# Eight block transfers replaced by two ScalarE copies in a gated delta rule kernel

## The reference

```
attn = -(einsum('bhcid,bhcjd->bhcij', k_beta, k) * decay_mask)   # 64x64 for each chunk and value head
attn = where(upper, 0, attn)                                     # strictly lower triangular
attn = scan(_correct_row, attn)                                  # rows 1..63: forward substitution
attn = attn + eye(64)                                            # = inverse of (1 - attn)
value_corrected = attn @ v_beta
for each chunk c:                                                # carries a 128x128 state
    v_prime = v_c - k_cumdecay_c @ state
    out_c   = (q_c @ state) * g_exp_c + intra_c @ v_prime
    state   = state * g_exp_last_c + (k_c * k_decay_c)^T @ v_prime
out = rmsnorm(out * silu(z)) @ W_out
```

## Time and profile before

| | |
|---|---|
| median of 3 runs | 4948.56 us (4940.16 to 4948.61) |
| the profiled execution | 4963.24 us |
| its span, from first to last instruction | 4961.4 us |
| TensorE matmuls | 4639.9 us busy, 94% |
| VectorE | 3576.3 us busy, 72% |
| ScalarE | 3063.8 us busy, 62% |
| GpSimd | 693.1 us busy, 14% |
| mean granted TensorE clock | 0.984 |

### The profile page before, as it was taken

The page is one execution under the profiler, slowest core; times in us unless marked ns, Lnnn a source line. Parts: engine busy times, 40 slices in busy tenths (PEclk is TensorE's granted clock), DMA queues, the critical chain, the costliest instruction groups (busy, mean ns, idle before and its releaser), DMA issues.

```text
span 4961.4 us, 144941 instructions
## 1 busy us (share of the span) xinstructions
PE 4639.9 (94%) x54288; PEld 3178.9 (64%) x54320; DVE 3576.3 (72%) x7576; ACT 3063.8 (62%) x7979; POOL 693.1 (14%) x680
## 2 busy tenths in 40 slices
PE   4898999999999899999999899999999999999998
PEld 2555666666666566666666666666666666666666
DVE  7554777777777677777777677777777777777776
ACT  2333666666666566666666566666666666666665
POOL 0000111111111111111111111111111111111111
PEclk8999999999999999999999999999999999999999
DMA  2111222222223222222223222222223232222221
GB/s 61 32 43 60 66 69 52 61 67 61 68 50 81 69 68 50 64 67 61 59 58 81 68 58 59 64 63 65 60 57 81 68 69 55 59 66 60 69 58 34
DMA packets 760100, 305.22 MB, mean 62 GB/s; under 512 B 672880, under 2 KB 716016, under 8 KB 749168
## 3 DMA queue, kind: packets, MB, share of 16 engines
q1 hardware_dynamic: 620144, 287.40, 23.6%
q10 hardware_dynamic: 139264, 8.42, 1.8%
HBM read 216.96 MB, written 66.07 MB: 57 GB/s over the span
## 4 chain that ended last, share of the span: by engine, by line
PE 71%; DVE 8%; ACT 6%; issue 6%; SPq 5%; DMA 4%; ACTq 0%; DVEq 0%; POOL 0%; POOLq 0%
PE pj L660 16%; PE dsb L819 8%; PE pj L655 7%; PE pod L803 4%; PE pot L777 4%; PE dsb L791 4%; PE ms L693 4%; PE pot L748 4%; PE pod L760 3%; PE pj L650 3%; ACT arena L983 2%; PE pot L605 2%; PE ms L673 2%; SPq L333 2%; PE ms L687 2%
## 5 line engine op out<-in xcount | busy, mean ns | idle before, releaser
L660 PE MATMUL pj<-xnT,wt 128*128 128x512 f32 x2048 | 1023.2, 623 | 29.3 <-DMA cw<-in_L_attn_conv_weight 15.7
L1292 DVE SCALAR_TENSOR_TENSOR cy<-xpad,cw,cy 128x1024 f32<-128x1024 f32 x768 | 981.3, 1278 | 10.4 <-ACT cy L1003 1.2
L1562 POOL TENSOR_TENSOR rout<-rin,expo 128x2 f32<-128x2 f32 x512 | 358.3, 700 | 3743.4 <-DVE rin L1443 3743.4
L819 PE MATMUL dsb<-wo,yT 128*128 128x256 f32 x2048 | 575.7, 404 | 17.9 <-issue 16.9
L660 PEld LDWEIGHTS pj<-xnT,wt 128*128 128x128 f32 x2048 | 352.2, 192 | 358.9 <-issue 343.9
L1429 DVE SCALAR_TENSOR_TENSOR st<-st,gel,dsb 128x128 f32<-128x128 f32 x1536 | 430.4, 343 | 207.7 <-PE dsb L791 202.8
L1002 ACT ACTIVATE xpad<-pj 128x512 f32<-128x512 f32 x512 | 304.9, 596 | 360.8 <-PE pj L660 360.8
L655 PE MATMUL pj<-wt,xnT 128*128 128x256 f32 x2048 | 510.0, 392 | 0.0
L1062 ACT ACTIVATE yT<-dsb 128x256 f32<-128x256 f32 x512 | 202.2, 395 | 491.2 <-PE dsb L810 489.5
L819 PEld LDWEIGHTS dsb<-wo,yT 128*128 128x128 f32 x2048 | 348.7, 190 | 123.2 <-issue 95.4
L655 PEld LDWEIGHTS pj<-wt,xnT 128*128 128x128 f32 x2048 | 368.9, 190 | 84.0 <-issue 44.3
(11 more groups left out here) (174 smaller groups left out, 8011.6 us busy)
## 6 DMA issues: line engine op xcount, KB each, us to landing
qge<-ge_rows SPq DMA_DIRECT2D x64, 1024.0 KB, 7.4
wt<-in_L_attn_W_qkvz SPq DMA_DIRECT2D x64, 768.0 KB
gb<-g_rows SPq DMA_DIRECT2D x128, 256.0 KB
a_d<-at SPq DMA_DIRECT2D x64, 512.0 KB, 2.6
wo<-in_L_attn_W_out SPq DMA_DIRECT2D x64, 256.0 KB, 2.7
x_d<-xpair SPq DMA_DIRECT2D x128, 128.0 KB, 1.8
ap_<-a_d SPq DMA_DIRECT2D x512, 16.0 KB, 1.8
dd<-x_d SPq DMA_DIRECT2D x512, 16.0 KB, 2.1
```

The lines of the kernel that those rows point to most:

```text
L660: last = mm(pj[n % 2][:, :], wt[:, k, col:col + DH], batch(xnT, k, i), start=(k == 0), stop=(k == KD - 1))
L819: last = mm(dsb[:, 0, GRP * DH:GRP * DH + D], yT[:, h, :], wo[:, p, h, :], start=(h == 0), stop=(h == GRP - 1))
L1292: stt(y, x[:, :, tap:tap + SEQ], cw[:, kind, tap:tap + 1], y, ALU.mult, ALU.add).then_inc(S["conv"], 1)
L1562: tt(rout[:, :], rin[:, :], expo[:, 0, 0:GRP], ALU.pow).then_inc(S["routs"], 1)
```

## The change

The eight transfers into `eturn` and their semaphore go. ScalarE fills `eturn` with two copies out of `ee` instead, each from one half of the partitions into the other, 8 units of 64. They stand at s = 19 between the second and the third negation, behind a wait for the transfers into `ee`, which ScalarE did not wait for until now. TensorE's round 0 waits for the copies in place of the transfers.

```diff
@@ relayout_back (SyncE)
                 blocks_back(sp, 0, dd, d_dd)
-                loaded(sp, d_x1, g, 1)
-                apart(sp)
-                for r in range(GRP * NBLK):
-                    turned = (r + NBLK) % (GRP * NBLK)
-                    sp.dma_start(eturn[turned * BLK:(turned + 1) * BLK, :, (r % NBLK) * BLK:(r % NBLK + 1) * BLK],
-                                 x_d[r * U + U // 2:(r + 1) * U, 1].rearrange("u j i -> j u i")).then_inc(d_et, 16)
@@ fixpoint (TensorE)
                     loaded(pe, d_ee, g, GRP * NBLK)
-                    loaded(pe, d_et, g, GRP * NBLK)
+                    after(pe, "turned", g, NB)
                     after(pe, "pneg", g, 2)
@@ ScalarE
+            def turned_blocks(g):
+                loaded(act, d_ee, g, GRP * NBLK)
+                for b in range(NB):
+                    fn(eturn[half(1 - b), :, :], ee[half(b), 8:16, :], ACT.Copy).then_inc(S["turned"], 1)
@@ front_piece (ScalarE)
-                for n in range(3):
-                    if s == 19:
-                        negated(g, n)
+                if s == 19:
+                    negated(g, 0)
+                    negated(g, 1)
+                    turned_blocks(g)
+                    negated(g, 2)
```

More of the change, by code:

```diff
@@ L205, in build @@
         d_w, d_g, d_ge, d_wo, d_q = sem("d_w"), sem("d_g"), sem("d_ge"), sem("d_wo"), sem("d_q")
-        d_a0, d_a, d_off, d_x0, d_x1, d_dd, d_ee, d_et = (sem(n) for n in ("d_a0", "d_a", "d_off", "d_x0", "d_x1", "d_dd", "d_ee", "d_et"))
+        d_a0, d_a, d_off, d_x0, d_x1, d_dd, d_ee = (sem(n) for n in ("d_a0", "d_a", "d_off", "d_x0", "d_x1", "d_dd", "d_ee"))
         phase = sem("phase")
@@ L231, in build @@
             counted(name, n)
-        for name, n in (("pcopy", RING), ("silu", 4), ("sqs", 2), ("dexp", 1), ("pneg", 3), ("wev", NC), ("wos", 1),
+        for name, n in (("pcopy", RING), ("silu", 4), ("sqs", 2), ("dexp", 1), ("pneg", 3), ("turned", NB), ("wev", NC), ("wos", 1),
                         ("sso", NC), ("yte", NC), ("ysc", NC)):
@@ L887, in _ @@
         def _(act):
-            starts(act, ("pcopy", "silu", "sqs", "dexp", "pneg", "wev", "wos", "sso", "yte", "ysc"))
+            starts(act, ("pcopy", "silu", "sqs", "dexp", "pneg", "turned", "wev", "wos", "sso", "yte", "ysc"))
             fn = nc.scalar.activation
```

## The result

| | before | after |
|---|---|---|
| median, measured in turn | 4944.36 us (6 runs, 4935.2 to 4953.43) | 4967.85 us (6 runs, 4951.0 to 4977.76) |
| ratio, 95% interval | | 1.0043 [1.0027, 1.0058] |
| span of the profiled execution | 4961.4 us | 4976.0 us |
| mean granted TensorE clock | 0.984 | 0.983 |

The change made the kernel 0.43% slower, by about 21 us, where 25 us less had been forecast. So the loss is small but stands.

A forecast was written before the change was run, and what follows sets the result against it. TensorE, busy 94% of the span, was taken as the bound, idling on eturn's transfers before the first round. Gains of 15.4 and 11.0 less 1.0 us gave 25, so 4924 us on the median; 8-in-10 range 4908 to 4952.

The forecast's parts named there:

- the moved wt load: SyncE's queue: next head's wt load issues 5 us earlier, beside the last ee blocks; no gain by itself.
- the sum: First-round starts over 64 heads: 15.4 + 11.0 - 1.0 + 0 = 25.4 us gained, taken as 25.
- rival 1: ee lands late behind wt, decisive beyond 2.3 us later; slower, 4958 to 4984 us; chance 0.10.
- ScalarE's wait for ee: New wait before the copies: least margin 1.6 us, median 2.3 over 64 heads, so no cost.
- The pair of copies: ScalarE, SBUF to SBUF: pair ends 1.05 us behind the second negation, bounds 0.96 and 1.26 us.
- The release: TensorE's way from released wait to the first round's first matmul: 0.34 us, 0.09 in the last 14 heads.
- rival 4: All idle time VectorE had before its residual goes: 33.7 us gained, 4915 us; chance 0.09.
- rival 3: Small gain: copies or release slower, or time waited out at TensorE's next stop; 4938 us up; 0.24 with rival 5.
- which wait stood in front of the first round: TensorE before the first round waits for eturn's transfers: 49.3 us idle in 40 waits.
- ScalarE's later work has cover: Work queued behind the copies comes 1.05 us later, covered by 3.29 us of ScalarE's idle time in head 7; no cost.
- rivals 2 and 5: 2: ScalarE becomes the bound, 67 us, 5016, chance 0.05; 5: transfers were hidden anyway, chance folded into rival 3.
- rival 5: The eturn transfers in front of the first round were hidden anyway; chance folded into rival 3, together 0.24.

The follow-up runs named there:

- e16: The changed kernel unaltered, run again on the chip of e17, against the kernel before: 4971.06 us, ratio 1.0041.
- e17: The changed kernel with wt issued at its old time, behind the second negation (e9 once more), against the kernel before: 4938.34 us, ratio 0.9982.
- e8: The changed kernel without ScalarE's copies and TensorE's wait for them, wt still early, part of the inverse left out, against the kernel before: 4951.82 us, 1.0019.
- e12: e9 without both copies and the wait for them, wt at its old time, against the kernel before: 4933.42 us, ratio 0.9967.
- e9: The changed kernel with wt held behind ScalarE's second negation, its old time, against the kernel before: 4929.6 us, ratio 0.9979.
- e2: The kernel before, eturn transfers kept, with wt issued between the dd blocks and eturn's, against the kernel before: 5064.42 us, ratio 1.0227.
- e1: The changed kernel with SyncE issuing wt only once the ee blocks have landed, against the kernel before: 4956.31 against 4950.22 us, ratio 1.002.
- e10: The kernel before with ScalarE's two copies added, into a tile nobody reads, eight transfers kept, against the kernel before: 4940.23 us, ratio 0.9993.

## Why the prediction was wrong

**The step that failed** is the moved wt load. The prediction says that "it moves forward by 5 us", that "the earlier load gains nothing by itself" and that this "is where this change could bite", and gives it no term in the sum. It has one: e16 against e17 prices it at +33 us, more than the whole forecast gain. It acts in two ways.

*The late ee blocks (rival 1).* The mechanism was named, with a chance of 0.10, and ScalarE's wait for ee was "costed at nothing". "wt lasts 3 us in all" was read as a reason against it; it is about the size of the delay. The last ee block of a head came 2.5 us later in the median, just past the rival's threshold of 2.3: 4.62 us with 768 KB beside it, 3.46 with 384, 2.0 with none. The Trainium skill, "DMA: Bandwidth & Descriptors", section "Queues, rings and completion order", has a DMA engine take turns between SP's and ACT's rings at packet borders only; the delays agree with blocks that stand behind wt's share. Their price is an estimate. By the idle time before the first round it is 11 us (e16 less e17). By the ratios it is 6 us (0.24% from e8 to the change, less 0.12% from e12 to e9), a difference that the intervals don't resolve.

*TensorE's pauses and its clock.* No rival spoke of them. Against e12, e8 has the same work and waits and only wt earlier: 1.0019 [1.0003, 1.0036] against 0.9967 [0.9953, 0.9982], 26 us, of which late ee blocks hold 1.2. TensorE stops at fixed places of the code: the pauses of over 1 us in pj<-dd,off stand in heads 3, 10, 11, 18, 19, 26, 27, 34, 35, 42 and 43, before and after the change alike, so at four heads of the loop's body of 16, pass after pass. They lasted 1.0 to 2.1 us before, 1.6 to 3.0 after, 1.0 to 1.8 in e9, 2.1 to 3.3 in e2. After the change, the granted clock went to 1.2 GHz behind 7 of the 9 that were over 2 us long; before, behind the 2 longest, of 2.09 us. The profile of before showed these waits, 18.1 us of them, and the prediction passed over them as they weren't eturn's.

*What TensorE waits for there* can be read from the DMA packets in the traces. The page of either kernel has a queue of instruction reads, 16 KB each:
```profile
q8 instruction: 455, 7.45, 0.6%
```
One such read comes for every 251 matmuls and weight loads of TensorE (median, before), and its pauses end with them. Over the 17 traces there are 328 pauses of TensorE of over 1 us, from 545 us on, without a releaser and in the middle of a batch or in pj<-dd,off. All 328 end 1.0 to 1.7 us behind the end of a read on this queue. By chance about one in ten would (an estimate: 436 reads in 4416 us). So, as far as the traces can tell, TensorE waits there for its own instructions. In pj<-dd,off the read starts 0.8 us ahead of the stop before (median), 0.8 to 1.0 in e1, e9, e12 and e17. It starts 0.0 us ahead of it after, 0.2 in e8 and e16, and 0.2 behind it in e2. In these four runs, with wt early, every one of the 42 reads starts between 0.7 us ahead of the end of wt's last packet and 0.2 us behind it, 3.7 to 4.4 us behind the issue of wt. In before and e17 all 21 start ahead of wt's issue, by 0.2 to 2.4 us. The early load thus holds up the read, TensorE stops for longer, and more often its clock falls.

**The pair of copies.** Forecast: ends 1.05 us behind the second negation, bounds 0.96 and 1.26. Measured: the pair takes 1.28 us and ends 1.30 us behind it where ee is there in time. In head 7 after:
```profile
1006.22 1.07 ACT L1032 ACTIVATE pbd<-ms 128x512 f32<-128x512 f32 x2
1007.32 1.28 ACT L1039 ACTIVATE eturn<-ee 64x512 f32<-64x512 f32 x2
...
1008.51 0.57 ACT L1032 ACTIVATE pback<-pj 128x512 f32<-128x512 f32 x1
```
From the negation's end at 1007.29 to 1008.60. The overlap of 0.1 us that two negations show does not come between the two copies, of 0.628 us each, nor between negation and copy, so the pair lies beyond my upper bound. It isn't the shape: the two activations of that shape in the earlier trace rows do overlap, in the kernel before.
```profile
161.63 0.63 ACT L926 ACTIVATE kq<-vT 64x512 f32<-64x512 f32 x1
162.16 0.61 ACT L927 ACTIVATE kq<-vT 64x512 f32<-64x512 f32 x1
```
Why the copies don't stays open. By the prediction's own method the longer pair alone takes 26.0 to 15.0 us; with ee 2.5 us later besides, 5.7 are left, still a gain. The release was right: the first matmul at 1008.95, 0.35 us later (0.34 forecast).

**What a microsecond at the first round is worth.** The sum took each as one microsecond of the kernel if VectorE could follow. e9 gave 0.2%, 10 us, of the 15; e12 gave 16 us for an idle time of 52, where rival 4, fed by what VectorE idled, had 33.7. The rest is idled again in rounds 1 and 2, as rival 3 said of "TensorE's next stop", but for the most part no other engine makes that stop: a TensorE that waits less comes sooner to the end of the instructions that it has. All pauses in the middle of a batch, over 0.2 us long, are 52.4 us in e12 and 20.7 in e9, and all 98 of them (72 and 26) end 1.0 to 1.75 us behind an instruction read. So even with wt in place the forecast of 25 would have been more than twice too high, and rival 3 would have come.

**Right:** which wait stood in front of the first round; that ScalarE's later work has cover (e10); that rivals 2 and 5 are out (rival 5 narrowly, as e9 gains 0.2%); the 128 activations, and wt issued 5 us earlier.

**The sum.** On the medians: -10 us for the freed wait (e9), +33 for the early load (e16 against e17), +23; measured +21 to +24. By the estimates above the 33 split into some 6 to 11 us for late ee blocks and 22 to 27 for the pauses and the clock.

**What stays open.** That TensorE's long pauses end behind instruction reads, and that the reads start only as wt's last packets end, is seen in every case of the traces. No run moved the code against the load or the reads to another time, so the order of cause rests on these times and on e16 against e17. Why the clock falls behind some pauses and not behind others of the same length isn't shown. Why halving wt at its old place gives 0.43% was not taken apart further; its profile has about 21 us less idle time from 545 us on, spread over many places.

## What to carry to other kernels

Taking transfers off a queue moves everything behind them forward; price the next large load at its new time as carefully as the work removed, and hold it back with a wait of its own if small transfers, or the instruction reads of an engine that never rests, share its new place. Pauses without a releaser at the same places of a loop are worth a look before the change: here they were on the page and took the gain. Look at the last block of a group, not at the median of all, when something waits for the whole group. An idle time before one stage of a chain is an upper bound of its worth: here 52 us of it were worth 16.

## What the runs showed of the hardware

- The last of eight 16 KB blocks on ScalarE's queue came 2.5 us later (median) beside a 768 KB load on SyncE's, and 1.35 us later beside 384 KB.
- TensorE pauses in the middle of batches whose operands are there, in pj<-dd,off at the same places of a loop body in each pass. Each of the 328 pauses without a releaser of over 1 us in these traces ended 1.0 to 1.7 us behind a 16 KB read on the queue of instruction reads. Beside an early 768 KB load the read started about 0.8 us later, at the end of the load, and the pauses in pj<-dd,off grew from 1.7 to 2.3 us (medians, before and after). Behind 7 of 9 pauses of 2.1 to 3.0 us the granted clock stood at 1.2 GHz, for 3.4 us or in one case 6.8.
- ScalarE's two copies of 64x512 from SBUF to SBUF (0.628 us each) did not overlap; two other activations of that shape, and two 128x512 copies out of PSUM (0.584 us), did, by 0.1 us. The same 64x512 copy took 0.422 us on VectorE and 1.69 us on GpSimd as a product.
